# GNN layer with a routed feed-forward: base rows stored to the output, attention rows added there by accumulating scatters

## The reference

```python
xn = _layernorm(x)
x = x + gnn(xn, edges) + mix(xn)           # first sum
x = x + ffn(_layernorm(x))                 # second sum
```

## Time and profile before

| | |
|---|---|
| median of 3 runs | 2846.49 us (2846.21 to 2849.05) |
| the profiled execution | 2847.4 us |
| its span, first to last instruction | 2846.2 us |
| mean granted clock of PE | 0.881 |
| busy share PE, DVE, ACT, POOL | 74%, 84%, 36%, 74% |
| HBM read, written | 519.06 MB, 71.84 MB |

### The profile page before, as it was taken

How to read it: one execution, slowest core, us unless ns; L and a number is a source line. 1 busy time by engine, 2 the same in 40 slices (tenths; PEclk the granted TensorE clock), 3 DMA queues, 4 the chain that set the end, 5 groups by cost and what they waited for, 6 DMA issues and landing times. The chain is left out here.

```text
span 2846.2 us, 36156 instructions
## 1 busy us (share of the span) xinstructions
PE 2110.9 (74%) x9360; PEld 1696.3 (60%) x9361; DVE 2397.0 (84%) x3259; ACT 1029.1 (36%) x4377; POOL 2103.6 (74%) x2223
## 2 busy tenths in 40 slices
PE   6976777766667777688888776666656637599998
PEld 5764566655556666466666554444444427499997
DVE  6867999988889999999999888899999956366765
ACT  4434666656566666211111111011111106345453
POOL 6767777777777777777777777777777765578785
PEclk9988999999998898889999877778787875699999
DMA  7769777777777777888888877777777749333331
GB/s 239 267 230 322 219 219 218 218 219 217 218 219 218 218 218 213 249 230 255 261 257 255 247 224 211 211 211 211 211 210 211 211 159 293 107 77 89 80 90 15
DMA packets 257952, 586.96 MB, mean 206 GB/s; under 512 B 49583, under 2 KB 135678, under 8 KB 257722
## 3 DMA queue, kind: packets, MB, share of 16 engines
q0 software_dynamic: 150448, 467.11, 58.4%
q1 hardware_dynamic: 98135, 109.52, 11.7%
q10 hardware_dynamic: 9296, 9.44, 1.0%
HBM read 519.06 MB, written 71.84 MB: 208 GB/s over the span
## 5 line engine op out<-in xcount | busy, mean ns | idle before, releaser
L1036 POOL DMA_INDIRECT wide<-kv_d,arena x1099 | 1052.4, 958 | 339.7 <-issue 326.4
L1333 PE MATMUL ps<-wide,arena 128*128 128x264 f32 x2432 | 698.9, 450 | 232.4 <-DVE wide L1435 232.2
L1333 PEld LDWEIGHTS ps<-wide,arena 128*128 128x128 f32 x2432 | 534.1, 225 | 389.1 <-DVE wide L1435 275.6
L1036 POOL DMA_INDIRECT arena<-kv_d,arena x539 | 515.2, 956 | 164.3 <-issue 160.0
L1171 ACT ACTIVATE ps<-wide 128x256 f32 x229 | 88.8, 388 | 1267.3 <-DVE arena L1401 1263.7
L1404 DVE TENSOR_REDUCE arena<-arena 128x64 f32<-128x2048 f32 x229 | 523.9, 2288 | 7.9
L1333 PE MATMUL ps<-arena 128*128 128x264 f32 x1216 | 350.4, 451 | 132.6 <-DVE arena L1435 132.4
L1401 DVE TENSOR_TENSOR arena<-wide,ps 128x2048 f32<-128x2048 f32 x153 | 349.5, 2284 | 88.1 <-DMA wide<-kv_d,arena 88.0
L1333 PEld LDWEIGHTS ps<-arena 128*128 128x128 f32 x1216 | 266.7, 225 | 212.8 <-DVE arena L1435 157.5
L140 PE MATMUL ps<-halves 128*128 128x256 f32 (+2 forms) x2304 | 362.1, 319 | 3.2 <-DVE halves L1696 1.6
L1435 DVE TENSOR_TENSOR wide<-wide,ps 128x2112 f32<-128x2112 f32 x152 | 356.8, 2347 | 0.0
(11 more groups left out here) (338 smaller groups left out, 3096.9 us busy)
## 6 DMA issues: line engine op xcount, KB each, us to landing
wide<-kv_d,arena POOLq DMA_INDIRECT x1099, 3.8
arena<-in_w SPq DMA_DIRECT2D x16, 1024.0 KB, 5.5
kv_d<-wide SPq DMA_DIRECT2D x49, 260.0 KB
arena<-xn_d SPq DMA_DIRECT2D x82, 128.0 KB, 3.5
arena<-kv_d,arena POOLq DMA_INDIRECT x539, 3.8
hb_d<-arena SPq DMA_DIRECT2D x16, 516.0 KB, 6.1
xn_d<-arena SPq DMA_DIRECT2D x7, 896.0 KB
base_d<-arena ACTq DMA_DIRECT2D x49, 128.0 KB, 3.5
```

What stands on the lines that cost most here:

```text
L1036: e.indirect_dma_start(out=kvb[k][:, j, :], out_offset=None, in_=kv_d, in_offset=bass.IndirectOffsetOnAxis(ap=ixb[k][:, j:j + 1], axis=0)) ...
L1333: m = e.matmul(psE[(k + 1) % 3][:, 0:264], ident, kvb[b][:, j, 256:ROW], start=(j == 0), stop=(j == J - 1))
```

## The change

`base_d` and `at_d` are gone. ACT stores the base rows to their rows of `out`; the tail tile with its 106 valid rows is the first of them. POOL waits for these stores (`e_bs`) and then adds the attention rows to `out` by 49 accumulating scatters with a bounds check, since places beyond row 6,249 have no row there. SP loads the sums from `out` into `XH[:, :, 0:256]`. The loads of base rows, the sum on DVE and the stores of sums are gone, as are the waits for `t_o`. In the tail tile the 22 places without a row are filled from `x`. A late tile adds the difference to what was added for it first (a subtraction on DVE, counted by `l_df`).

```diff
@@ attention_in, base_in
         def attention_in(grp):
-            t_x2[grp] = dma(Y, XH[:, tiles_of(grp), 0:256], at_d[grp * 896:grp * 896 + 896, :].rearrange("(t p) d -> p t d", p=128), s_x2[grp])
-
-        def base_in(grp):
-            n_, r0, c0 = (7 if grp < 6 else 6), grp * 896 + 128, place(7 * grp)
-            t_x2[grp] = dma(Y, XH[:, c0:c0 + n_, 256:512], base_d[r0:r0 + 128 * n_, :].rearrange("(t p) d -> p t d", p=128), s_x2[grp])
+            n_, r0, c0 = (7 if grp < 6 else 6), grp * 896, place(7 * grp)
+            t_x2[grp] = dma(Y, XH[:, c0:c0 + n_, 0:256], out[r0:r0 + 128 * n_, :].rearrange("(t p) d -> p t d", p=128), s_x2[grp])
             if grp == 6:
-                t_x2[grp] = dma(Y, XH[:, place(48), 256:512], base_d[0:128, :], s_x2[grp])
+                dma(Y, XH[0:N - 48 * 128, place(48), 0:256], out[48 * 128:N, :], s_x2[grp])
+                t_x2[grp] = dma(Y, XH[N - 48 * 128:128, place(48), 0:256], x[0:NP - N, :], s_x2[grp])
@@ SP, end of the block
             s_we[0].inc(e.dma_start(w1r, kpart(w1[0])), 16)
-            base_in(0)
-            base_in(1)
             e.wait_ge(s_ag.h, 16 * NT)
@@ GpSimd, late_tile
-                e.wait_ge(l_ao, ld)
+                e.wait_ge(l_df, ld)
                 e.nop().then_inc(e_dm, 1)
-                e.indirect_dma_start(out=at_d, out_offset=bass.IndirectOffsetOnAxis(ap=permc, axis=0), in_=o_row, in_offset=None
-                                     ).then_inc(l_sc, 16)
+                e.indirect_dma_start(out=out, out_offset=bass.IndirectOffsetOnAxis(ap=permc, axis=0), in_=o_row, in_offset=None,
+                                     bounds_check=N - 1, oob_is_err=False, compute_op=ALU.add).then_inc(l_sc, 16)
@@ GpSimd, behind the gathers
             e.wait_ge(s_in[3].h, 16)
+            for k in range(RING):
+                e.wait_ge(e_bs[k], 16 * (AUX + (k == RING - 1)))
             for c in range(NT):
                 e.wait_ge(e_ao, c + 2)
-                e.indirect_dma_start(out=at_d, out_offset=bass.IndirectOffsetOnAxis(ap=sortedi[:, c, 0:1], axis=0),
-                                     in_=qs[:, c, :], in_offset=None).then_inc(s_ag.h, 16)
+                e.indirect_dma_start(out=out, out_offset=bass.IndirectOffsetOnAxis(ap=sortedi[:, c, 0:1], axis=0), in_=qs[:, c, :],
+                                     in_offset=None, bounds_check=N - 1, oob_is_err=False, compute_op=ALU.add).then_inc(s_ag.h, 16)
@@ ScalarE, base_out
-                e.dma_start(base_d[bass.ds(val(e, u, 48 * 128), 128), :], xm[k]).then_inc(e_bs[k], 16)
-                e.reg_add(u, u, 128)
+                if tail:
+                    e.dma_start(out[48 * 128:N, :], xm[k][0:N - 48 * 128, :]).then_inc(e_bs[k], 16)
+                else:
+                    e.dma_start(out[bass.ds(val(e, u, 47 * 128), 128), :], xm[k]).then_inc(e_bs[k], 16)
+                    e.reg_add(u, u, 128)
@@ VectorE, late_tile
                 divide(mo[0], l_fin)
+                e.wait_ge(e_ao, NT + 1)
+                e.nop().then_inc(e_dm, 1)
+                e.wait_ge(l_ao, ld)
+                e.tensor_tensor(o_row, o_row, qsf[:, bass.ds(val(e, tl, NT - 1) * QI, 256)], ALU.subtract).then_inc(l_df, 1)
@@ second stage, loads
         for grp in range(2, 7):
             attention_in(grp)
-            base_in(grp)
@@ spread2
             part = XH[:, tiles_of(grp), :]
-            t_sum[grp] = v(V.tensor_tensor(part[:, :, 0:256], part[:, :, 0:256], part[:, :, 256:512], ALU.add))
-            wait(V, t_sum[grp])
             for i in range(7):
@@ out_group and its call, once per group
-            wait(Y, t_sum[grp])
-            if grp < 6:
-                return dma(Y, out[grp * 896:(grp + 1) * 896, :].rearrange("(t p) d -> p t d", p=128), XH[:, tiles_of(grp), 0:256], s_o)
...
-                t_o = out_group(grp)
@@ load_r
-            wait(Y, t_sc, t_o, t_xp.get(e - 2), *t_y.get(e - 2, ()))
+            wait(Y, t_sc, t_xp.get(e - 2), *t_y.get(e - 2, ()))
```

More of the change, by code:

```diff
@@ L117, in gps_layer_kernel @@
         xn_d = dram("xn_d", [NP, D])
-        base_d = dram("base_d", [NP, D])
-        at_d = dram("at_d", [NP, D])
         hb_d = dram("hb_d", [H * CP, HR])
@@ L873, in gps_layer_kernel @@
         e_so, e_si, e_sa, e_sd, e_se, e_sl, e_sg = [esem(n) for n in ("so", "si", "sa", "sd", "se", "sl", "sg")]
-        l_fin, l_tp, l_at, l_wo, l_ao, l_sc = [esem(n) for n in ("lfin", "ltp", "lat", "lwo", "lao", "lsc")]
+        l_fin, l_tp, l_at, l_wo, l_ao, l_df, l_sc = [esem(n) for n in ("lfin", "ltp", "lat", "lwo", "lao", "ldf", "lsc")]
         XH = R12[:, 0:NT * XW].rearrange("p (t w) -> p t w", w=XW)
@@ L1114, in tile_end, with base_out @@
                     e.reg_add(o_at, o_at, QI)
-            def base_out(k):
+            def base_out(k, tail=False):
                 e.reg_add(bc, bc, 1)
@@ L1179, in _, with body @@
             indices(0)
-            def body(k, mix=False, join=None, aux=False, i=0):
+            def body(k, mix=False, join=None, aux=False, i=0, tail=False):
                 record()
@@ L1195, in body @@
                 if aux:
-                    base_out((k - 2) % RING)
+                    base_out((k - 2) % RING, tail)
             def first_out():
                 for k in range(RING):
-                    body(k, aux=k > 0)
+                    body(k, aux=k > 0, tail=k == 1)
             def last_out():
@@ L1532, in gps_layer_kernel @@
         void = R3[:, 4400:4401]
-        t_sum = {}
         wait(V, t_fin)
@@ L1548, in gps_layer_kernel @@
         t_rt = [None]
-        s_o, s_sc = sem("s_o"), sem("s_sc")
+        s_sc = sem("s_sc")
         def seq(ins):
@@ L1660, in scale2 @@
             return v(V.scalar_tensor_tensor(out=nms[grp % 2], in0=r3(mvs[grp % 2], 2)[:, :, 0], scalar=-1.0, in1=r, op0=ALU.mult, op1=ALU.mult))
-        def out_group(grp):
-            wait(Y, t_sum[grp])
-            if grp < 6:
-                return dma(Y, out[grp * 896:(grp + 1) * 896, :].rearrange("(t p) d -> p t d", p=128), XH[:, tiles_of(grp), 0:256], s_o)
-            dma(Y, out[grp * 896:grp * 896 + 768, :].rearrange("(t p) d -> p t d", p=128), XH[:, place(42):place(48), 0:256], s_o)
-            return dma(Y, out[48 * 128:N, :], XH[0:N - 48 * 128, place(48), 0:256], s_o)
         def center_h(u):
@@ L1773, in gps_layer_kernel @@
         turn(0, 1)
-        wait(V, t_sc, t_o)
+        wait(V, t_sc)
         t_pad = v(V.memset(u1[:, 0:8 * (CP - CE)], 0.0))
@@ L1779, in gps_layer_kernel @@
         t_hs = {}
-        wait(S, t_bb, t_sc, t_o)
+        wait(S, t_bb, t_sc)
         wait(V, t_bb)
-        wait(G, t_o, t_sc)
+        wait(G, t_sc)
         for e in range(8):
@@ L1845, in gps_layer_kernel @@
                 t_y[e] = [t_yq[z] for z in range(4 * e, q + 1)]
-        wait(Y, *[(s_, s_.n) for s_ in s_ye], (s_o, s_o.n), (s_ed, s_ed.n), (s_pz, s_pz.n), (s_hz, s_hz.n),
+        wait(Y, *[(s_, s_.n) for s_ in s_ye], (s_ed, s_ed.n), (s_pz, s_pz.n), (s_hz, s_hz.n),
              (s_ag, s_ag.n), (s_sc, s_sc.n), (s_q, s_q.n), *[(s_, s_.n) for s_ in s_st])
```

## The result

The changed kernel takes 2861.14 us (median of 5 runs, 2860.09 to 2864.69) against 2846.21 (5 runs, 2842.81 to 2849.05): a ratio of 1.0058, 95% interval 1.0044 to 1.0072, or 12.5 to 20.5 us more, centre 16.5. Forecast were 20.1 more. It is slower, for the reason forecast, by somewhat less at the centre; the interval just takes in the forecast.

What follows compares the result with a forecast made beforehand. GpSimd's issue of 49 attention scatters, then of `hb_d` scatters, was taken to bound the affected stretches. +28.4 for accumulation less 8.3 for removed sums gave +20.1, from the 2846.5 median 2866.6 us; 8-in-10 range 2859 to 2878.

Steps and rivals of the forecast that it cites:

- The scatters' price: Attention scatters at the edge loop's end: 1.85 us an issue when accumulating, +28.4 us in all, all on the path.
- the overlaps with VectorE: Attention scatters running beside VectorE's last edges: stretching them adds 0.9 us in all.
- the last landing: End of the row of attention scatters: the last accumulating one takes 2.7 us to land, the shortest seen; median 3.8.
- B: Rival on the attention scatters: accumulation is free, only the gain is left, 2838 us; chance 0.06.
- C: Rival in the edge loop: VectorE holds accumulating scatters up, or each costs the median or more; 2871 to 2889 us; chance 0.09.
- E: Rival on the attention scatters: accumulating DMAs back up in the DMA queues; +71 us and more, 2909 up; chance 0.03.
- The barrier, costed at 0: Between the attention scatters and second stage: barrier and loads of groups 0 and 1 follow the landing as before, 0.
- The stage's gain: Second normalisation and routing: without VectorE's sums it gets 8.3 us shorter.
- group 0's sum: Start of the second stage: this sum stands in front of everything; its removal gives -2.2 us.
- the unbroken run of 35 scatters: GpSimd's scatters to `hb_d` from 2404.36 us: one stretched by meeting a sum no longer is, -1.2 us.
- D: Rival on the second stage: it doesn't give back, gain only 3.4 us, 2871.5 us; chance 0.07.
- The slack of 1.2 us for the fourth batch: Second stage: the fourth batch's slots are still ready before GpSimd is through the third, with 1.2 us left.

Runs made afterwards that it cites:

- after_plain: Changed kernel with its 49 attention scatters plain instead of accumulating (base rows left out of the result): 2836.17 us, ratio 0.9971 to the kernel before the change.
- after_sum: Changed kernel with seven VectorE sums of the same shape put back in the same place, results unused: 2871.68 us, ratio 1.0095 to the kernel before the change.
- after_traffic: Changed kernel with as many bytes loaded and stored as before, without sums: 2863.40 us, ratio 1.0062 to the kernel before the change.
- before_early: Kernel before the change with the sums of groups 2 to 6 moved earlier in VectorE's queue: 2841.70 us, ratio 0.9983.
- before_seven: Kernel before the change with seven routes, each group routed by itself: 2840.38 us, ratio 0.9975.
- before_load_add: Kernel before the change with seven routes, base rows of groups 2 to 6 added in SBUF by six accumulating direct DMAs from GpSimd: 2841.25 us, ratio 0.999.
- before: The kernel without the change: 2846.21 us, median of 5 runs.
- after: The kernel with the change, nothing else altered: 2861.14 us, ratio 1.0058 to the kernel without it.

## Why the prediction was right

**The scatters' price.** Right: 1.848 us an issue against 1.85, taken from the expert scatters' row. The accumulation makes it (`after_plain`). Of the smaller terms two were off, and cancel by luck: the overlaps with VectorE cost nothing instead of 0.9, and the last landing took 3.5 instead of 2.7, nearer the median that I had set aside. 92.24 came out for 92.4. B, C and E are refuted by the same rows: the price is not free, no scatter takes over 1615 ns, and the 49 land at 3.8 in the median. (E's price was also summed wrongly: 49 x 2.7 less 64.0 is 68, not 71. Nothing rests on it.)

**The barrier, costed at 0.** The one step that failed, by 2.1 us: the prediction let the barrier follow the landing, "as before". SP's load to VectorE's first instruction fell from 7.24 to 5.10. Counted from the end of GpSimd's last scatter, VectorE starts after 7.1 us instead of 8.7, which is 1.6 of the 2.1; the other 0.5 is the later landing (2.0 instead of 1.5 after that end), which SP's load waits for and the barrier doesn't. The trace of before had the row of 8.7, and I didn't read it. That the accumulation makes it shorter is shown (`after_plain` has 8.7), and that late tiles have no part in it; how it does so isn't known.

**The stage's gain.** 8.3 forecast, 10.2 measured, of which 2.1 are the barrier; the stage proper gave 8.1, in these parts: VectorE's first instruction to ScalarE's first centring, where group 0's sum stood, 6.90 to 5.11, -1.8 (forecast -2.2); from there to the third batch's first scatter 47.05 to 41.93, -5.1 (forecast -4.85); from there to SP's load of `hb_d`, with the unbroken run of 35 scatters, 47.30 to 46.11, -1.2 (forecast -1.2). That the sums did it, and not the transfers, is shown from both sides: a sum put back costs 8.2 of stage (`after_sum`), the transfers put back cost nothing (`after_traffic`). D is refuted. The slack of 1.2 us for the fourth batch held, to 0.1.

**The sum.** With the barrier, +28.2 - 10.2 = +18.0 by the profiles, +16.5 by the runs with 12.5 to 20.5 about it; forecast +20.1. 2.1 of the difference are the barrier. The other 1.5, between profiles and runs, is inside the interval. The end of the kernel costs nothing, as said (-0.3), and no cost of the base stores shows beside the edge loop.

**Where the gain went.** It is real and as large as worked out, 8 us; the change pays for it with 0.57 us on each of 49 instructions, on the engine that had no cover. Part of it can be had without the accumulation: `before_early` (ratio 0.9983), and `before_seven` (0.9975) by another way, make the kernel faster.

## What to carry to other kernels

Before moving an add into a DMA, look at who issues it and what covers that engine: a price of half a microsecond an instruction came to 28 us in a row of 49 that everybody waits for. (No run here tests what it costs beside other work.) Work that is "removed" from a busy engine is worth only what others waited for: here 1.8 us in front of the stream, three stalls of TensorE and one stretched scatter. Stalls can often be had by moving the work in the queue. When a producer's batches gate an issuing engine, read which batch comes last, since splitting only the first of two equal ones moves the wait and not the end.

## What the runs showed of the hardware

- An accumulating scatter of 128 rows of 1 KB costs 1.54 us to issue against 0.97 for a plain one to the same rows, lands in 3.8 instead of 2.4, and loads the 16 DMA engines more: a share of 0.64 at 78 GB/s beside the last edges, against 0.32 at 111 for the plain one. An estimate from these: 0.64 x 1.85 = 1.2 us of all sixteen engines a scatter, against 0.32 x 1.28 = 0.4.
- The bytes counted as read from memory are 512.64 MB with accumulation and without it (`after_plain`): what the accumulation reads of its target does not appear in that count, though the DMA share shows its time.
- Direct accumulating transfers into SBUF, issued together, landed one behind the other, about 7.6 us apart for 896 rows of 1 KB or 1.1 us per 128 rows, beside SP's stores (`before_load_add`: landings from 14.1 us after the first issue at 2362.6 to 38.7 after the last at 2368.3).
- A plain `hb_d` scatter of 0.98 us took 2.14 to 2.76 us where it met a VectorE sum with both inputs in SBUF, and ended 0.85 to 0.87 us after it (four times in `before`; it came back in `after_sum`).
- From the end of GpSimd's last scatter to its first instruction behind the end of the block it took 8.7 us with plain scatters (`before`, `after_plain`) and 7.1 with accumulating ones (`after`, `after_sum`).
